# The recurrence's input weights prepared first, and the last expert group summed by VectorE

## What is computed

```python
def step(carry, xs):                       # recurrence, 256 steps
    h, c = carry
    xi_t, xf_t, xg_t, xo_t = xs            # x @ U + b, for all steps
    i_t = sigmoid(xi_t + h @ V_i)
    g_t = tanh(xg_t + h @ V_c)
    o_t = sigmoid(xo_t + h @ V_o)
    c_new = h * c + i_t * g_t
    h_new = o_t * tanh(c_new)
...
h1 = einsum('bsd,edh->bseh', x, w1)        # experts
h2 = einsum('bsd,edh->bseh', x, w2)
expert_out = einsum('bseh,eho->bseo', silu(h1) * h2, w3)
out = einsum('bseo,bse->bso', expert_out, dispatch)
```

## Time and profile before

| | us |
|---|---|
| median of 3 runs | 1346.93 |
| lowest and highest run | 1344.14 and 1347.83 |
| the profiled execution, its own time | 1337.93 |
| its span, first to last instruction | 1336.1 |
| busy: TensorE / VectorE / ScalarE / GpSimd | 1023.1 / 846.9 / 516.2 / 273.9 |
| mean granted clock of TensorE | 0.782 |

### The profile page before, as it was taken

The page is one execution under the profiler, slowest core; times in us unless marked ns, Lnnn a source line. Parts: engine busy times, 40 slices in busy tenths (PEclk is TensorE's granted clock), DMA queues, the critical chain, the costliest instruction groups (busy, mean ns, idle before and its releaser), DMA issues. The chain is left out here.

```text
span 1336.1 us, 27269 instructions
## 1 busy us (share of the span) xinstructions
PE 1023.1 (77%) x9646; PEld 588.6 (44%) x9646; DVE 846.9 (63%) x2450; ACT 516.2 (39%) x1332; POOL 273.9 (21%) x376
## 2 busy tenths in 40 slices
PE   6878886577888756666666666666973999999996
PEld 2366652253666434454544444443541333333332
DVE  6686746745556465555555555555356788888885
ACT  3543433353443322222223222323542554455452
POOL 4504003200000000000000000000100355555556
PEclk9889998878999955555555555557995999999998
DMA  7000002000000000000000000000001755555550
GB/s 230 1 1 1 1 2 79 0 1 0 1 0 1 1 1 1 0 0 0 0 0 0 0 0 0 0 0 1 0 1 36 170 130 118 124 134 119 119 134 9
DMA packets 10675, 47.39 MB, mean 35 GB/s; under 512 B 1520, under 2 KB 5744, under 8 KB 6128
## 3 DMA queue, kind: packets, MB, share of 16 engines
q1 hardware_dynamic: 10608, 46.49, 14.2%
HBM read 43.86 MB, written 2.62 MB: 35 GB/s over the span
## 5 line engine op out<-in xcount | busy, mean ns | idle before, releaser
L1636 PE MATMUL wide<-ls_h,ls_v 128*128 128x16 f16 x2304 | 105.1, 176 | 145.2 <-DVE ls_h L1735 141.8
L2145 ACT ACTIVATE ex_gated<-wide,unscale 128x1024 f32<-128x1024 f32 x128 | 142.2, 1114 | 139.7 <-PE wide L2111 139.5
L2161 DVE TENSOR_TENSOR ex_hid<-wide,ex_gated 128x1024 f32<-128x1024 f32 x128 | 155.9, 1223 | 39.4 <-ACT ex_gated L2145 28.0
L1636 PEld LDWEIGHTS wide<-ls_h,ls_v 128*128 128x128 bf16 x2304 | 82.0, 106 | 214.2 <-DVE ls_h L1735 214.1
L2087 POOL TENSOR_TENSOR ex_acc<-ex_part,ex_acc 128x512 f32<-128x512 f32 x120 | 152.6, 1272 | 94.7 <-DVE ex_part L2177 80.5
L1725 DVE TENSOR_TENSOR_SCAN ls_cells<-ls_terms 128x48 f32<-128x48 f32 x256 | 73.8, 288 | 123.6 <-ACT ls_terms L1660 123.6
L1660 ACT ACTIVATE ls_terms<-wide 128x32 f32<-128x32 f32 x256 | 54.3, 212 | 229.4 <-PE wide L1641 229.4
L2123 PE MATMUL wide<-ex_hid,w 128*64 128x512 f32 x512 | 116.7, 598 | 0.0
L2111 PE MATMUL wide<-xh,wh 64*128 64x512 f16 x512 | 99.1, 383 | 5.2 <-PEq L81 3.7
L2111 PE MATMUL wide<-xl,wh 64*128 64x512 f16 x512 | 98.3, 380 | 0.0
L2111 PE MATMUL wide<-xh,wl 64*128 64x512 f16 x512 | 98.2, 380 | 0.0
(11 more groups left out here) (368 smaller groups left out, 1882.4 us busy)
## 6 DMA issues: line engine op xcount, KB each, us to landing
ex_d<-route SPq DMA_DIRECT2D x64, 512.0 KB, 6.4
par_attn<-in_attn SPq DMA_DIRECT2D x1, 2704.0 KB, 13.6
par_rest<-in_rest SPq DMA_DIRECT2D x1, 2523.5 KB, 18.9
L_xin<-in_x SPq DMA_DIRECT2D x8, 256.0 KB, 5.7
w<-in_w SPq DMA_DIRECT2D x1, 2048.0 KB, 8.2
out<-ex_acc SPq DMA_DIRECT2D x16, 128.0 KB, 3.3
w<-in_w SPq DMA_DIRECT2D x1, 512.0 KB, 9.1
route<-ro_dt SPq DMA_DIRECT2D x2, 256.0 KB, 2.0
```

The lines of the kernel that those rows point to most:

```text
L1636: pe.matmul(ig[:, g, :] if g < 2 else o, vp[part][:, g, :], h1[:], start=False, stop=False, skip_group_check=True)
L2145: act.activation(gated[:, n % 2, :], pair_of_up(n // GS, 2 * (n % GS))[:], ACT.Silu, scale=m.unscale[:, 0:1]).then_inc(s["gated_ready"], 1)
L2161: dve.tensor_tensor(hid[:, n % (2 * GS), :], pair_of_up(n // GS, 2 * (n % GS) + 1)[:], gated[:, n % 2, :], ALU.mult).then_inc(s["hid_ready ...
```

## The change

In the recurrence's preparation, the three scalings into `u` and the one into `bias` come first, and `u_ready` is raised by the scaling into `bias` itself. The three scalings into `vs`, the split and the memsets follow. TensorE waits for `u_ready` alone ahead of the five parts, and for `zeros` behind them.

In the expert stage, GpSimd's adds of the last tile stop after 12 of 16 experts. For the last group VectorE weighs the two pairs into the two halves of `gated`, which nothing else uses any more, and then sums them by itself: the two pairs (1024 columns), the two experts that remain (512 columns), and that sum onto `acc` (512 columns). The last instruction raises `acc_ready` by four, so that the store's condition stays the same.

```diff
             pe.wait_ge(s["u_ready"], 1)
-            pe.wait_ge(s["zeros"], 1)
             for part in range(5):
                 prepare(0, 0, part)
+            pe.wait_ge(s["zeros"], 1)
...
-            for g, n in enumerate("gio"):
-                half = 1.0 if n == "g" else 0.5
+            halves = [(g, n, 1.0 if n == "g" else 0.5) for g, n in enumerate("gio")]
+            for g, n, half in halves:
                 dve.tensor_scalar(u[:, g, :], p[f"u_{n}"], half, None, ALU.mult)
-                dve.tensor_scalar(vs[:, g, :], p[f"v_{n}"], half / SC, None, ALU.mult)
-
-            link(dve.tensor_scalar(bias[0:3, :], p["lstm_b"][0:3, :], p["lstm_half"][0:3, :], None, ALU.mult))
+            dve.tensor_scalar(bias[0:3, :], p["lstm_b"][0:3, :], p["lstm_half"][0:3, :], None, ALU.mult)\
+               .then_inc(s["u_ready"], 1)
+            for g, n, half in halves:
+                ins = dve.tensor_scalar(vs[:, g, :], p[f"v_{n}"], half / SC, None, ALU.mult)
+            link(ins)
...
-            dve.sem_inc(s["u_ready"], 1)
...
-                for e in range(E):
+                for e in range(E if t < TILES - 1 else E - GS):
...
-            for r in range(2):
-                weigh(NG - 1, r)
+            def weigh_last(r):
+                dve.wait_ge(s["down_done"], 2 * NG - 1 + r)
+                if r == 0:
+                    dve.wait_ge(s["hid_ready"], TILES * E)
+                    dve.wait_ge(d_landed[(NG - 1) % GT], 32 * TILES)
+                dve.scalar_tensor_tensor(gated[:, r, :].rearrange("p (e n) -> p e n", e=2),
+                                         pair_of_down(NG - 1, r)[:].rearrange("p (e n) -> p e n", e=2),
+                                         m.unscale[:, 0:1], d[:, (NG - 1) % GT, 2 * r:2 * r + 2, :], ALU.mult, ALU.mult)\
+                   .then_inc(s["last_step"], 1)
+
+            weigh_last(0)
+            weigh_last(1)
+            whole = gated[:, 0, :]
+            dve.wait_ge(s["last_step"], 2)
+            dve.tensor_tensor(whole, whole, gated[:, 1, :], ALU.add).then_inc(s["last_step"], 1)
+            dve.wait_ge(s["last_step"], 3)
+            dve.tensor_tensor(whole[:, 0:TW], whole[:, 0:TW], whole[:, TW:2 * TW], ALU.add).then_inc(s["last_step"], 1)
+            dve.wait_ge(s["last_step"], 4)
+            dve.wait_ge(s["acc_ready"], E * TILES - GS)
+            last = acc[:, (TILES - 1) % 2, :]
+            dve.tensor_tensor(last, last, whole[:, 0:TW], ALU.add).then_inc(s["acc_ready"], GS)
```

More of the change, by code:

```diff
@@ L2037, in expert_stage @@
         s = {n: sem(n) for n in ("warm", "up1_done", "up2_done", "gated_ready", "hid_ready", "down_done",
-                                 "part_ready", "acc_ready", "xh_ready", "xl_ready")}
+                                 "part_ready", "acc_ready", "last_step", "xh_ready", "xl_ready")}
         d_landed = [sem(f"d_landed{q}") for q in range(GT)]
```

## The result

| | before | changed |
|---|---|---|
| median, us (8 runs each) | 1345.77 | 1339.01 |
| lowest to highest, us | 1342.66 to 1348.53 | 1330.17 to 1342.78 |
| ratio to before, 95% interval | | 0.9945 (0.9919 to 0.9972) |
| measured again later on one chip, median (22 and 12 runs) | 1347.38 | 1341.06 |
| ratio of that, 95% interval | | 0.9949 (0.9930 to 0.9969) |

A forecast was written before the change was run, and what follows sets the result against it. The prediction saw a string of stages with no engine busy throughout, TensorE waiting for VectorE before the recurrence and GpSimd's adds bounding the end. 1346.93 less 3.1 + 3.1 = 6.2 us gave 1340.7 us, range 1336.5 to 1345.8.

The forecast's parts named there:

- The sum: Whole kernel: 3.1 us saved at the recurrence's start plus 3.1 at the program's end, 6.2 us, taken from 1346.93.
- the entry: VectorE's first memset of the recurrence's stage to TensorE's first recurrent weight load; forecast 4.3 us, 7.40 before.
- the end: TensorE's last weight load of the program to issue of the last stores, 8.45 us before; forecast 3.1 us shorter.
- Part one: Recurrence's preparation: with u and bias scaled first, TensorE starts its five parts earlier, saving 3.1 us.
- The lag from there to TensorE: Recurrence's preparation: an increment on the bias instruction itself reaches TensorE's next load in 0.13 us, against 0.27 for bare increments.
- The wait for zeros: Behind TensorE's five parts: met at 480.89 us, 0.3 us before TensorE comes to it, so it costs nothing.
- the cap that the prediction had named: Recurrence's preparation: VectorE's memsets, done at 480.62 plus a lag of 0.27 us, limit the gain to 3.39 us.
- Part two: Last expert group: four GpSimd adds go, VectorE sums instead, and the store is issued at 1329.10 instead of 1332.18, saving 3.1 us.
- The wide sum: VectorE's 128x1024 sum at the program's end: held by GpSimd's fourth add, ending 1.08 us after it, at 1327.62 us.
- That only one end gains: Rival, chance 0.12: either the recurrence's start or the program's end gives nothing, so the time is 1343.8 us.
- VectorE's sum does not get ahead of GpSimd's add: Rival at the program's end, chance 0.06: VectorE's 128x1024 sum goes before GpSimd's fourth add, costing 0.2 us, 1340.9 us.
- The clock: Rival, chance 0.05: TensorE's granted clock is slower than before, costing 9.9 us, so the time is 1350.6 us.

## Why the prediction was right, point by point

**The sum.** 6.2 us were forecast, 3.1 for each part; the entry gained 3.21 and the end 3.02, and the medians moved by 6.8 and 6.3. The time of 1340.7 came out as 1339.01 and, again, 1341.06. That it came so near is in part luck: it starts from the median of three runs, 1346.93, where eight have 1345.77, and the spread of runs is larger than the error.

**Part one.** Bias as the fourth instruction was to start 0.47 us after the first memset, and does (480.57 - 480.10). The lag from there to TensorE was the mis-sized term: I took 0.13 us from the recurrence's h, and it is 0.05 (480.84 to 480.89), so the gain was 0.1 us larger. The five parts took 3.40 us, against 3.39, with the clock at 0.50 on all sides. The wait for zeros was to cost nothing with 0.3 us to spare; VectorE ends 0.45 us ahead, which less the lag of 0.27 leaves 0.18, since TensorE started 0.1 us sooner than forecast. The experiment with the wait put back shows that this is the step on which all of part one rests, and the version with u and bias a stage earlier meets the cap that the prediction had named.

**Part two.** The weighings stand 1.71 us apart and wait for TensorE alone. The wide sum was expected to be blocked by GpSimd's last add, to take 1.48 us and to end 1.08 behind it, and takes 1.50 and ends 1.08 behind it; with one GpSimd add less it takes 1.23. The narrow sums take 0.69 us each. One step was 0.06 us short: ahead of the last sum stand two waits and the gap is 0.10 us instead of 0.04 (1329.77 to 1329.87). The last chain puts 0.04 of it down to VectorE's queue at L2207, the second wait; no run here removes that wait. It is why the end gained 3.02 us and not 3.08.

**The rivals.** That only one end gains has fallen by the runs of each part. VectorE's sum does not get ahead of GpSimd's add: the add starts at 1326.70 us, 0.85 us ahead of it. The clock is real as a source of spread, with 9.0 us between executions at the mark ahead of the recurrence, but in both directions and for every kernel; the two columns outside the change moved the profiled spans by 4.6 us against it, and a dozen runs average over that. The rival that something such as the loading of its instructions holds TensorE back at 477.8 us has fallen as well: its first load stands 0.05 us behind bias. Of the signs, the step of the recurrence is unchanged; its mean is 1.67 us, where the prediction had read 1.65 from one step.

**What the prediction left open.** It could not say why the profiled execution before lay 9 us below the median. The stages now place them. Against the changed kernel measured again, whose profiled execution is close to its median, the one before is 8.8 us shorter ahead of the recurrence: 5.6 in the slice attention, 3.9 in the windowed attention, 1.1 and 0.9 in the two convolution stages, less 2.6 in the three stages in which it was slower. Another 1.4 us lie behind the recurrence. Most of this goes with the time at 1.2 GHz; why the clock differs between executions stays open. Carrying the difference over unchanged was the right choice. Had I started from the profiled execution's time, the forecast would have been 1331.7 us, 7.3 below the first median and 9.4 below the second.

## What to carry to other kernels

At the edge of a stage, look for work that waits for a counter which stands for more than that work needs: one counter for "inputs scaled" and another for "all buffers ready" gave 3.2 us for a few moved lines, because a chain of dependent steps, 424.8 us long before and after, passed it on in full. At the end of a program, count what remains on each engine once the last matmul is done and give the rest to the one with the least left, but let VectorE's sums of two SBUF inputs overlap a busy GpSimd by one instruction at most. For gains below a per cent, compare distances between marks within a stage first and the medians of a dozen runs after that; two profiled spans alone would have shown 1.6 us here, a quarter of what the change is worth.

## What I had not expected of the hardware

An increment on a VectorE instruction reached TensorE's next weight load in 0.05 us here and takes 0.13 us in the recurrence. Two waits in a row ahead of a VectorE instruction went with a gap of 0.10 us, one with 0.04. And issuing the last two stores from two queues at the same moment, 0.60 and 0.75 us long instead of 1.25 us for both in a row, shortened the tail by 0.2 us only: the second store was issued 0.64 us sooner and landed 0.2 us sooner. A VectorE sum of two SBUF inputs and a GpSimd add took turns whole, but for some 0.15 us at each change.
